# Dense Gelu experts in float32: block products of a chunk pair by seven multiplications, token group outermost

## What is computed

```python
logits = xf @ gate_w.T + gate_b
logits = logits * jax.lax.rsqrt(ms + eps) * rms_w
gates = jax.nn.softmax(logits / TEMPERATURE, axis=-1)
norm_g = masked / (masked + 1e-06)
h = jax.nn.gelu(jnp.einsum('nd,edh->neh', xf, w1) + b1, approximate=False)
y = jnp.einsum('neh,ehd->ned', h, w2) + b2
out = (y * norm_g[:, None, None]).sum(axis=1)
```

## Time and profile before

| | |
|---|---|
| median of 3 runs | 3260.92 us (3253.55 to 3262.09) |
| the profiled execution, own time | 3263.56 us |
| its span | 3262.3 us |
| TensorE matmuls busy | 3072.1 us (94%) |
| TensorE weight loads busy | 2141.3 us (66%) |
| VectorE busy | 1869.3 us (57%) |
| ScalarE busy | 1181.3 us (36%) |
| GpSimd busy | 624.0 us (19%) |
| mean granted TensorE clock | 0.982 |
| chain that ended last, by engine | PE 78%, DVE 11%, ACT 4%, issue 3%, POOL 2%, DMA 2% |

### The profile page before, as it was taken

One profiled execution on the slowest core, in us unless ns is written; L12 is line 12 of the kernel. 1 busy time (PEld: TensorE's weight loads), 2 busy tenths in 40 slices (PEclk: granted clock), 3 DMA queues, 4 the chain that ended last, 5 costly groups with the idle time before them and its releaser, 6 DMA issues.

```text
span 3262.3 us, 40086 instructions
## 1 busy us (share of the span) xinstructions
PE 3072.1 (94%) x15200; PEld 2141.3 (66%) x15200; DVE 1869.3 (57%) x3285; ACT 1181.3 (36%) x2206; POOL 624.0 (19%) x998
## 2 busy tenths in 40 slices
PE   7999999999999999999999999879998898997996
PEld 5778877677767776776666666556666664555664
DVE  5996789558856875685311101794317767774113
ACT  4443323552354336322221222241224336662331
POOL 1306401100100010002100000241343222112554
PEclk9999999999999999999999999999999999998998
DMA  5200000010002001100100000002451011112633
GB/s 137 65 1 1 29 26 1 13 56 13 1 13 67 1 1 34 46 1 1 39 13 26 14 1 1 20 1 104 167 193 45 4 47 50 35 41 97 219 123 107
DMA packets 85396, 151.03 MB, mean 46 GB/s; under 512 B 26357, under 2 KB 62743, under 8 KB 80471
## 3 DMA queue, kind: packets, MB, share of 16 engines
q1 hardware_dynamic: 70327, 77.15, 7.7%
q0 software_dynamic: 14880, 71.33, 6.3%
HBM read 173.14 MB, written 17.56 MB: 58 GB/s over the span
## 4 chain that ended last, share of the span: by engine, by line
PE 78%; DVE 11%; ACT 4%; issue 3%; POOL 2%; DMA 2%; SPq 0%; ACTq 0%; DVEq 0%; POOLq 0%
PE psum L420 9%; PE psum L443 8%; PE psum L1760 7%; PE psum L1748 7%; PE psum L1422 7%; PE psum L1434 6%; PE psum L2249 6%; PE psum L2270 3%; PE psum L410 2%; PE psum L456 2%; PE psum L1117 2%; PE psum L2424 2%; PE psum L2853 2%; PE psum L728 1%; DVE row L621 1%
## 5 line engine op out<-in xcount | busy, mean ns | idle before, releaser
L420 PE MATMUL psum<-Vt,shared 128*128 128x256 f32 (+1 forms) x1600 | 361.6, 381 | 0.4
L443 PE MATMUL psum<-Kt,xnTt 128*128 128x512 f32 (+1 forms) x960 | 343.9, 508 | 0.5 <-ACT xnTt L528 0.5
L420 PEld LDWEIGHTS psum<-Vt,shared 128*128 128x128 f32 (+1 forms) x1600 | 297.8, 190 | 39.2 <-issue 1.2
L443 PEld LDWEIGHTS psum<-Kt,xnTt 128*128 128x128 f32 x960 | 179.9, 190 | 158.0 <-issue 153.1
L1434 PEld LDWEIGHTS psum<-expert_w,prep 128*128 128x128 f32 x1024 | 194.6, 190 | 78.1 <-issue 57.9
L1434 PE MATMUL psum<-expert_w,prep 128*128 128x256 f32 x1024 | 240.7, 379 | 0.0
L1422 PE MATMUL psum<-weights,expert_w 128*128 128x512 f32 x512 | 240.3, 593 | 0.0
L3111 DVE CUSTOM_DVE_ANT_0 psum<-psum,expert_w 128x128 f32<-128x128 f32 (+7 forms) x256 | 191.9, 775 | 76.5 <-PE psum L2853 73.3
L1322 DVE SCALAR_TENSOR_TENSOR bias<-Kt,small,bias 128x1232 f32<-128x1232 f32 x96 | 149.2, 1554 | 129.7 <-ACT Kt L1306 128.4
L1780 ACT ACTIVATE prep<-psum,fside 128x512 f32<-128x512 f32 x128 | 88.0, 687 | 344.9 <-PE psum L1748 344.9
L1808 DVE TENSOR_TENSOR inner<-psum,inner 128x512 f32<-128x512 f32 x56 | 36.1, 686 | 308.2 <-PE psum L1760 308.2
(11 more groups left out here) (419 smaller groups left out, 6087.0 us busy)
## 6 DMA issues: line engine op xcount, KB each, us to landing
expert_w<-in_L_xattn_Wf SPq DMA_DIRECT2D x16, 512.0 KB, 5.6
weights<-q_parts SPq DMA_DIRECT2D x32, 144.0 KB
weights<-k_parts SPq DMA_DIRECT2D x96, 48.0 KB
weights<-in_L_xattn_Wk SPq DMA_DIRECT2D x4, 1024.0 KB, 4.9
weights<-in_L_xattn_Wv SPq DMA_DIRECT2D x4, 1024.0 KB, 7.0
weights<-in_L_xattn_Wq SPq DMA_DIRECT2D x4, 1024.0 KB, 5.4
weights<-in_L_xattn_Wo SPq DMA_DIRECT2D x4, 1024.0 KB, 5.3
weights<-in_L_ffn_w SPq DMA_DIRECT2D x8, 512.0 KB, 4.6
```

The costliest lines, as they stand in the source:

```text
L420: ins = pe.matmul(o_bank(t), probT[0:rows, t % 2, c, :], Vt[0:rows, t // TB, c, :], start=(c == 8), stop=(c == 7))
L443: ins = pe.matmul(flat[:, par * 3 * BANK + at:par * 3 * BANK + at + cols], xnTt[:, par, k, :], Kt[:, t // TB, k, src:src + cols], start=(k ...
```

## The change

The experts go group outermost: a *turn* is one group with one expert (32 turns), a *set* is half a turn: two hidden chunks with 512 tokens (64 sets). Weights are loaded again in every turn, 32 MB in place of 8.

In a set both products are products of 2 x 2 blocks, done by the seven products of Strassen's scheme in Winograd's form. The first: 2 chunks x 2 halves of the width, times 2 halves of the width x 2 halves of the group; seven matmuls of 256 columns (`pe_set_first`). The second: 2 halves of the group x 2 chunks, times 2 chunks x 2 halves of the output width; seven products of two matmuls with 128 columns (`pe_set_second`, for the set before).

- GpSimd makes four sums and differences of the first weights and four of the second in every turn (`pool_mix_weights`, 8 operations of 128 x 256). `mixed` counts the halves.
- VectorE makes four of the tokens for every group (`dve_mix_rows`), puts the products together in six operations (`dve_set_products`: three partial sums and three blocks of the hidden chunks; ScalarE copies product 1 to SBUF for it first, since product 2 is then added onto the same bank), and makes four sums of the Gelu results in four more (`dve_set_sums`). `set_step` counts.
- ScalarE applies Gelu in three operations (256, 256 and 512 columns).
- The seven sums of the second product stay in PSUM banks 4 to 7 over all 8 experts of a group. Then ScalarE copies them to SBUF in four operations (`act_take_group`), GpSimd puts them together in seven operations and adds the bias of 1024 columns in an eighth (`pool_group_rows`), and VectorE multiplies by the gate in sets 4 to 7 of the next group, for the last group before tile 2 of the attention. The 64 additions of VectorE (L1808) are gone.
- The end of the decoder's last layer (adding its last group, statistics, normalising, new rows) goes in between the first eight sets on VectorE. The small uses of a bank go behind the second products of given sets (`BESIDE_SETS`) and share bank 3 with product 4; products 1 and 2 are in bank 0, 6 and 7 in bank 1, 5 and 3 in bank 2.
- Some semaphores of the set-up are joined; they count the same events.

The core of the diff (its removed functions stand in the code above):

```diff
+    TURNS_OF_EXPERTS = NG * E
+    SETS_OF_GROUP = E * FC // 2
+    SETS = NG * SETS_OF_GROUP
+    FIRSTS, MADES, STEPS_OF_SET = 5, 4, 5
+    FIRSTS_EXPERTS = STEPS * LAYERS + FIRSTS * SETS
+    HIDS_EXPERTS = STEPS * LAYERS + MADES * SETS
+    USED_EXPERTS = STEPS * LAYERS + SETS
+    ACCS_EXPERTS = NG * LAYERS + NG * 4
+    HALF_G = GRP // 2
...
+    def pe_set_first(pe, s):
+        n, q, g = s // 2, s % 2, s // SETS_OF_GROUP
+        w, m = raw_first(n), mix_slot(n)
+        def product(i, lhs, rhs, start=True, stop=True):
+            return pe.matmul(product_of(i), lhs, rhs, start=start, stop=stop, skip_group_check=True)
+        if s % SETS_OF_GROUP == 0:
             pe.wait_ge(feed_kept, PAIRS * LAYERS + 2 * g + 2)
+            pe.wait_ge(x_mixed, g + 1)
+        if q == 0:
+            expert_weights_landed(pe, n)
+            pe.wait_ge(mixed, 2 * n + 1)
...
+            pe.wait_ge(hid_made, mades(s - 1, 2))
+        product(1, w[:, 0, q, 0, :], x_block(g, 0, 0), stop=False).then_inc(first_made, 1)
+        if s:
+            pe.wait_ge(set_step, steps_of(s - 1, 1))
+        product(6, m[:, 1, q, :], x_mix(g, 1))
+        product(7, m[:, 2, q, :], x_mix(g, 2)).then_inc(first_made, 1)
+        if s:
+            pe.wait_ge(set_step, steps_of(s - 1, 2))
+        product(5, m[:, 0, q, :], x_mix(g, 0))
+        product(3, m[:, 3, q, :], x_block(g, 1, 1)).then_inc(first_made, 1)
+        pe.wait_ge(hid_made, mades(s, 1))
+        product(2, w[:, 1, q, 0, :], x_block(g, 1, 0), start=False).then_inc(first_made, 1)
+        if s:
+            pe.wait_ge(set_step, steps_of(s - 1, 3))
+            if s - 1 in BESIDE_SETS:
+                pe_beside_kept(pe, BESIDE_SETS[s - 1])
+        product(4, w[:, 1, q, 1, :], x_mix(g, 3)).then_inc(first_made, 1)
+    def pe_set_second(pe, s):
+        n, q, g = s // 2, s % 2, s // SETS_OF_GROUP
+        w, m = raw_second(n), mix_slot(n)
+        begin, end = s % SETS_OF_GROUP == 0, s % SETS_OF_GROUP == SETS_OF_GROUP - 1
+        def product(i, lhs, rhs, start=False):
+            for t in range(2):
+                ins = pe.matmul(acc_of(i)[:, t * P:(t + 1) * P], lhs[:, t * P:(t + 1) * P], rhs,
+                                start=(begin and start and t == 0), stop=end, skip_group_check=True)
+            return ins
+        if q == 0:
+            pe.wait_ge(mixed, 2 * n + 2)
+        pe.wait_ge(hid_made, mades(s, 2))
+        if begin:
+            pe.wait_ge(acc_added, NG * LAYERS + 4 * g)
+        pe.wait_ge(hid_made, mades(s, 4))
+        product(1, hid_of(s, 0, 0), w[:, q, 0, 0, :], True)
+        product(2, hid_of(s, 1, 0), w[:, q, 1, 0, :])
+        product(4, hid_of(s, 1, 1), m[:, 7, q, :], True)
+        pe.wait_ge(set_step, steps_of(s, 4))
+        product(5, sum_of(s, 0), m[:, 4, q, :], True)
+        product(7, sum_of(s, 2), m[:, 6, q, :], True)
+        pe.wait_ge(set_step, steps_of(s, 5))
+        product(6, sum_of(s, 1), m[:, 5, q, :])
+        product(3, sum_of(s, 3), w[:, q, 1, 1, :]).then_inc(hid_used, 1)
+    def pe_sets(pe):
+        for s in range(SETS):
+            pe_set_first(pe, s)
+            if s:
+                pe_set_second(pe, s - 1)
+            else:
+                pe_ffn_second(pe, LAYERS - 1, STEPS - 1)
+            if s in BESIDE_SETS:
+                pe.wait_ge(set_step, steps_of(s, 3))
+                pe_beside_sets(pe, BESIDE_SETS[s])
+        pe_set_second(pe, SETS - 1)
...
+    def act_sets(act):
...
+            act.wait_ge(first_made, firsts(s, 1))
+            if s:
+                act.wait_ge(set_step, steps_of(s - 1, 1))
+            act.copy(corner, product_of(1)).then_inc(hid_made, 1)
+            act.wait_ge(first_made, firsts(s, 4))
+            if s >= 2:
+                act.wait_ge(hid_used, uses_of(s - 2))
+            else:
+                act.wait_ge(hid_used, STEPS * LAYERS - 1 + s)
+            act.activation(hid_of(s, 0, 0), product_of(2), ACT.Gelu, bias=bias_of[0]).then_inc(hid_made, 1)
+            act.wait_ge(set_step, steps_of(s, 2))
+            act.activation(hid_of(s, 0, 1), hid_of(s, 0, 1), ACT.Gelu, bias=bias_of[0]).then_inc(hid_made, 1)
+            act.wait_ge(set_step, steps_of(s, 3))
+            act.activation(set_rows[s % 2][:, 1, :], set_rows[s % 2][:, 1, :], ACT.Gelu, bias=bias_of[1]).then_inc(hid_made, 1)
...
+    def act_take_group(act, g):
+        act.wait_ge(hid_used, uses_of(SETS_OF_GROUP * (g + 1) - 1))
+        act.wait_ge(y_made, g)
+        for i, bank in enumerate(range(4, 8)):
+            cols = BANK if bank < 7 else HALF_G
+            act.copy(acc_rows[i][:, 0:cols], psum[:, bank, 0:cols]).then_inc(acc_added, 1)
...
+    def dve_set_products(dve, s):
+        u, v, w = partial
+        dve.wait_ge(first_made, firsts(s, 2))
+        dve.wait_ge(hid_made, mades(s, 1))
+        if s >= 2:
+            dve.wait_ge(hid_used, uses_of(s - 2))
+        elif s == 1:
+            dve.wait_ge(hid_used, STEPS * LAYERS)
+        dve.tensor_tensor(u, product_of(6), corner, ALU.add).then_inc(dve_step, 1)
+        after_u = vs()
+        dve.wait_ge(dve_step, after_u)
+        dve.tensor_tensor(v, product_of(7), u, ALU.add).then_inc(set_step, 1)
+        dve.wait_ge(first_made, firsts(s, 3))
+        dve.tensor_tensor(w, product_of(5), u, ALU.add).then_inc(dve_step, 1)
+        after_w = vs()
+        dve.wait_ge(set_step, steps_of(s, 1))
+        dve.tensor_tensor(hid_of(s, 1, 1), product_of(5), v, ALU.add)
+        dve.wait_ge(dve_step, after_w)
+        dve.tensor_tensor(hid_of(s, 0, 1), product_of(3), w, ALU.add).then_inc(set_step, 1)
+        dve.wait_ge(first_made, firsts(s, 5))
+        dve.tensor_tensor(hid_of(s, 1, 0), v, product_of(4), ALU.subtract).then_inc(set_step, 1)
+    def dve_set_sums(dve, s):
+        s1, s2, s3, s4 = (sum_of(s, i) for i in range(4))
+        dve.wait_ge(hid_made, mades(s, 3))
+        dve.tensor_tensor(s3, hid_of(s, 0, 0), hid_of(s, 0, 1), ALU.subtract)
+        dve.wait_ge(hid_made, mades(s, 4))
+        dve.tensor_tensor(s1, hid_of(s, 0, 1), hid_of(s, 1, 1), ALU.add).then_inc(set_step, 1)
+        dve.wait_ge(set_step, steps_of(s, 4))
+        dve.tensor_tensor(s2, s1, hid_of(s, 0, 0), ALU.subtract).then_inc(dve_step, 1)
+        dve.wait_ge(dve_step, vs())
+        dve.tensor_tensor(s4, hid_of(s, 1, 0), s2, ALU.subtract).then_inc(set_step, 1)
...
+        dve_mix_rows(dve, 0)
+        for s in range(SETS):
+            dve_set_products(dve, s)
+            if s == 0:
+                add_group(3)
+            dve_set_sums(dve, s)
+            last_group(s)
+            gating(s)
+            narrow(s)
+            if s in BESIDE_SETS:
+                beside(s)
+            g, at = s // SETS_OF_GROUP, s % SETS_OF_GROUP
+            if at == SETS_OF_GROUP - 3 and g < NG - 1:
+                dve_mix_rows(dve, g + 1)
+            if g and 4 <= at < 8:
+                dve_gated_rows(dve, TG * (g - 1) + at - 4)
+                if at == 7:
+                    dve_aggregate(dve, TG * (g - 1), TG * g)
+            if g and at == 13:
+                dve_root(dve, None, TG * (g - 1), TG * g)
...
+    def pool_mix_weights(pool, n):
+        m = mix_slot(n)
+        def then_wait(ins):
+            ins.then_inc(pool_step, 1)
+            pool.wait_ge(pool_step, gs())
+        expert_weights_landed(pool, n)
+        if n >= 2:
+            pool.wait_ge(hid_used, uses_of(2 * (n - 2) + 1))
+        a11, a12, a21, a22 = (raw_first(n)[:, k, :, c, :] for c in range(2) for k in range(2))
+        then_wait(pool.tensor_tensor(m[:, 0], a21, a22, ALU.add))
+        pool.tensor_tensor(m[:, 2], a11, a21, ALU.subtract)
+        then_wait(pool.tensor_tensor(m[:, 1], m[:, 0], a11, ALU.subtract))
+        pool.tensor_tensor(m[:, 3], a12, m[:, 1], ALU.subtract).then_inc(mixed, 1)
+        b11, b12, b21, b22 = (raw_second(n)[:, :, c, h, :] for c in range(2) for h in range(2))
+        then_wait(pool.tensor_tensor(m[:, 4], b12, b11, ALU.subtract))
+        pool.tensor_tensor(m[:, 6], b22, b12, ALU.subtract)
+        then_wait(pool.tensor_tensor(m[:, 5], b22, m[:, 4], ALU.subtract))
+        pool.tensor_tensor(m[:, 7], m[:, 5], b21, ALU.subtract).then_inc(mixed, 1)
...
+    def pool_group_rows(pool, g):
+        def then_wait(ins):
+            ins.then_inc(pool_step, 1)
+            pool.wait_ge(pool_step, gs())
+        first, second = group_y[:, 0:2, :, :], group_y[:, 2:4, :, :]
+        pool.wait_ge(acc_added, NG * LAYERS + 4 * (g + 1))
+        if g == 0:
+            pool.wait_ge(gating_back, 1)
+        then_wait(pool.tensor_tensor(acc_row(6), acc_row(6), acc_row(1), ALU.add))
+        pool.tensor_tensor(first[:, :, 0, :], acc_row(2), acc_row(1), ALU.add)
+        then_wait(pool.tensor_tensor(acc_row(7), acc_row(7), acc_row(6), ALU.add))
+        then_wait(pool.tensor_tensor(acc_row(6), acc_row(6), acc_row(5), ALU.add))
+        pool.tensor_tensor(first[:, :, 1, :], acc_row(3), acc_row(6), ALU.add)
+        pool.tensor_tensor(second[:, :, 0, :], acc_row(7), acc_row(4), ALU.subtract)
```

(23 more changed lines are left out.)

478 lines of the change are left out of this document (252 added, 226 removed).

## The result

| | before | after |
|---|---|---|
| median of the runs | 3257.24 us (3253.19 to 3262.09, 4 runs) | 3227.23 us (3223.1 to 3229.91, 4 runs) |
| the profiled execution, own time | 3263.56 us | 3223.1 us |
| its span | 3262.3 us | 3221.9 us |
| the experts stage | 455.8 us | 414.4 us |
| behind it, to the end | 1197.0 us | 1197.9 us |

The ratio is 0.9906, 95% interval [0.9889, 0.9922]. 3227 us was forecast. Timed again beside E1 to E3 the ratio was 0.9897 [0.988, 0.9914] (3225.38 against 3262.15 us).

A forecast was written before the change was run, and what follows sets the result against it. TensorE's matmuls, busy throughout the experts, were taken as the bound. -47.6 + 2 + 1.6 + 6 + 4 = -34.0 us from 3263.56 gives 3229.6, the median 2.6 lower: 3227 us; range 3213 to 3246.

The forecast's parts named there:

- TensorE, -47.6 us: Experts' matmuls: a set of 6.14 us replaces two steps of 6.887 us, 0.74 us less, times 64 sets.
- surcharge of the Trainium skill: Narrow matmuls: 25 ns on each of 28 records per set, 45 us in all; not carried into the sum.
- Rival (b): Experts' narrow matmuls bound by their weight loads, a set 8.3 us, 3367 us in all; chance 0.04.
- First eight sets, +2: VectorE's added work at the experts' start, some 4 us at once in the first two sets: +2 us (0 to 5).
- ScalarE at a group's end, +1.6: ScalarE's four bank copies delay the next set's product 1 copy by 0.5 us, three times: +1.6 us (0 to 3).
- GpSimd, +6: GpSimd's mixes and group rows, held by VectorE's sums, come late: 2 us for each of three groups (0 to 12).
- three forecast waits of TensorE for GpSimd: Sign to look for in the changed profile: TensorE waiting at sets 20, 36 and 52, some 2 us each.
- Rival (a): Experts: each GpSimd mix operation held for a whole VectorE sum, 9 to 10 us lost three times, about 3250 us; chance 0.11.
- these fit into 1.6 us per set plus the slack: VectorE's extra work beside the experts' sets fits, except some 4 us at once in the first two; least slack 3.8 us.
- Rival (c): VectorE becomes the experts' bound, 7.9 us per set, 3340 us; decides from 0.67 us per operation; chance 0.05.
- DMA and semaphores, 0: Experts: 24 MB more of weight loads, ordered six sets ahead, and joined semaphores with the same events cost 0.
- The end, +4: Behind the experts: longer copies, and 3.8 us of gated rows, statistics and aggregate before attention tile 2: +4 us (0 to 5).

The follow-up runs named there:

- E1: The change's frame without its seven products, both products of a set in full; ratio to the kernel before 0.9995 [0.9984, 1.0006].
- E3: The change with only the second product of a set by seven, the first in full; ratio to the kernel before 0.995 [0.9933, 0.9966].
- E2: The change with only the first product of a set by seven, the second in full; ratio to the kernel before 0.9935 [0.992, 0.995].
- E9: The changed kernel with bias addition in four, spreads one per set, ScalarE's group-end copies of banks 6 and 7 later; 3220.13 us, ratio to before 0.9887.
- E5: The changed kernel without GpSimd's eight weight mixes from turn 2 on; experts stage 410.84 us.
- E7: The changed kernel with GpSimd's bias addition in four instructions of 256 columns in place of one of 1024; experts stage 412.69 us.
- E12: The changed kernel with GpSimd's bias addition to a group's rows done twice; experts stage 417.60 us.
- E11: The changed kernel with one more VectorE operation of 128x256 in every set; experts stage 15.2 us more.
- E8: The changed kernel with two more VectorE operations of 128x256 in every set; experts stage 455.2 us, 40.8 more.
- E10: The changed kernel without the last group's four gated rows and statistics; third attention scores 7.36 us behind the second, fourth 10.07 behind the third.
- E4: The changed kernel once more without edit, for a second profile; experts stage 414.39 us.
- E6: The changed kernel with VectorE's eight spreads of keys and values in sets 38 to 45; experts stage 413.52 us.

## Why the prediction was right, term by term

- **TensorE, -47.6 us**: E2 and E3 show 47.2, and so does the prediction's own sum with the distances not rounded (0.2159 and 0.1117 us: a set of 6.149 us). The rate of narrow records, read from 22 records of an unrelated transposition and the gate's loads, held for changing weights. The surcharge of the Trainium skill (TensorE: Matmul & The Clock Gate, Back-to-back issue gap), which is given for bf16, does not show in these float32 records. Rival (b) falls.
- **First eight sets, +2**: 0.9, all in set 1.
- **ScalarE at a group's end, +1.6**: 0.31 + 0.31 + 0.80 = 1.4, in sets 17, 33 and 49, gone in E9 but for 0.1. The 0.55 us per copy of a bank stands in none of the rows, which have 0.589 for one; the four copies together took 1.84 us, not 2.0.
- **GpSimd, +6**: the size was over, 3.5 us, and the mechanism half wrong. The holding is there and mutual, as the rows said, and as the rule of the Trainium skill has it (GPSIMD Engine Reference, the table at its head). But I let it delay GpSimd and make TensorE wait for the mixes. The chain of mix 9, rows and half of mix 10 took 17.6 us, not 17.1 + 2.6, within the 18.4: mixes ran at 0.72 to 0.91 us, and only 3 of 243 at 1.0 or more. A mix that meets a running sum ends some 0.58 us behind it, so it is held for 0.29 us at most, not for the whole 0.43. None of the three forecast waits of TensorE for GpSimd is there. The side that came late was VectorE, whose sums doubled where they met a mix, and TensorE waited for its steps. E5 to E7 show the cause, E12 that the margin I worked out is real: 2.4 us more gave 1.67, so some 0.8 us of it was left. Rival (a) falls with it. It was also priced too high: its own operations add up to 9.6 + 11.3 + 4.8 = 25.7 us, not 28, and three losses of 7.3 us, without lateness carried on, make 3243 us, not 3250.
- **VectorE**: "these fit into 1.6 us per set plus the slack" counted every sum at 0.43. With holding VectorE is busy 82%, not 75. Rival (c) does not happen, but E11 puts it nearer than I had it: it was to use up the whole gain at 0.67 us for each of ten operations, 2.5 us more per set, and E8 used it up with 1.1 us more; E11's 0.6 us already cost 15.
- **DMA and semaphores, 0**: E1's stage is that of before.
- **The end, +4**: the first four scores on GpSimd take 38.7 us from the stage's end, 36.0 before: 2.75. Of that 1.25 lie before the first, where GpSimd's bias addition holds L615 for 2.66 us (1.44 before), and I had put that place at 0.3. The rest is 2.7 us of gated rows or clock, as E10 showed, less the 1.2 us that the lower clock cost the kernel before.

**Sum.** The stage was forecast at about 418 us and is 414.4. The spans of the profiled pair differ by 40.5 us: 41.4 from the stage, 0.9 given back behind it, less than 0.1 ahead of it. The medians differ by 30.0 and 36.8 us in two sets of runs, so single executions stray by more than the two terms I argued over. Behind the stage, where the first profile of the change has 1197.9 us, kernels that run the very same code there took 1196.0 (E11), 1196.3 (E5), 1198.0 (E4), 1204.9 (E8) and 1205.4 us (E6). E12, with the longer stage, took 3220.1 us in all, less than the change. Part of the stray is the granted clock: the same stretch behind the attention took 30.8 us at 0.78 in the change, and 26.6 in the execution before. The 5 to 11 us between the stage's 41.4 and the medians I could not place beyond the 2.75 us of the first four tiles; there is one profile of before, and that stays open.

That the median came out at 3227 us is partly luck. The forecast was a difference, -34.0 us, from a median of before of 3260.9. With a fourth run that median is 3257.2, 3.7 us lower; the stage was better than forecast by 3.4; and the rest gave back 11.4 us where the forecast had 4. The three cancel. In the second set of runs the rest is 4.6 us.

## What to carry to other kernels

Where TensorE alone sets the pace, a product scheme is worth its columns at the measured distance between starts, and the halves of such a change can be built apart and added; what they lack to the sum is the interaction. Price the helpers by the pair of engines: where VectorE and GpSimd both work from SBUF, here a VectorE sum that met a GpSimd operation took up to that operation's length longer (0.42 to 0.83, or to 2.32), and the GpSimd operation at most 0.29. Then look at both for lateness: here VectorE came late, to which the prediction had given 3.8 us of slack, and not GpSimd with its 1.2. Keep GpSimd's instructions short beside an engine that is waited for, and put extra work where the set has room, not where it fits the code.
